# Another order for the dense groups and the expert additions behind the last expert tile

## The reference

```python
xn = layernorm(x)                                     # no weights
h  = layernorm(xn) * g1 + b1
q, k, v = h @ Wq + bq, h @ Wk + bk, h @ Wv + bv       # 16 heads, 4 key/value heads of 8
attn = softmax(rope(q) @ rope(k).T / sqrt(8), window of 32 keys)
x1 = xn + (attn @ v) @ Wo + bo
ff = gelu((layernorm(x1) * g2 + b2) @ Wf1 + bf1) @ Wf2 + bf2     # dense part, 128 -> 512 -> 128
top two of eight experts by xn @ gate.T, weights mult from a jittered softmax
moe = sum over the two of mult * ((silu(xn @ w1[e].T) * (xn @ w3[e].T)) @ w2[e].T)
out = x + (x1 + ff) + moe
```

## Time and profile before

| | |
|---|---|
| median of 3 runs | 522.35 us (519.64 to 522.42) |
| the profiled execution | 519.14 us, span 517.3 us |
| busy, share of the span | TensorE 87%, VectorE 74%, ScalarE 48%, POOL 43% |
| mean granted TensorE clock | 0.927 of 2.4 GHz |
| chain of waits, whole span | TensorE 57%, issue 16%, ScalarE 14%, VectorE 10% |

### The profile page before, as it was taken

The page is one execution under the profiler, slowest core; times in us unless marked ns, Lnnn a source line. Parts: engine busy times, 40 slices in busy tenths (PEclk is TensorE's granted clock), DMA queues, the critical chain, the costliest instruction groups (busy, mean ns, idle before and its releaser), DMA issues.

```text
span 517.3 us, 11263 instructions
## 1 busy us (share of the span) xinstructions
PE 448.0 (87%) x3374; PEld 414.7 (80%) x3375; DVE 382.3 (74%) x1019; ACT 249.6 (48%) x532; POOL 225.0 (43%) x252
## 2 busy tenths in 40 slices
PE   3944976869999999999999999999999999997846
PEld 2834976869989898989898989998989778786533
DVE  6858773776877777777777787867878788577682
ACT  2592004545554555555546464555554564653302
POOL 3630012534555555555555555555544553033110
PEclk9975556998999999999999999999999999999788
DMA  7850022443444544444544343434340500001431
GB/s 221 223 184 0 1 89 80 134 133 103 139 149 123 158 119 151 126 149 120 153 128 154 118 156 116 151 118 155 120 121 2 164 2 0 2 1 61 123 101 41
DMA packets 33667, 56.77 MB, mean 110 GB/s; under 512 B 5967, under 2 KB 21203, under 8 KB 33505
## 3 DMA queue, kind: packets, MB, share of 16 engines
q1 hardware_dynamic: 28160, 47.22, 29.9%
q0 software_dynamic: 4608, 8.93, 5.8%
q10 hardware_dynamic: 864, 0.20, 0.2%
HBM read 47.94 MB, written 8.91 MB: 110 GB/s over the span
## 4 chain that ended last, share of the span: by engine, by line
PE 57%; issue 16%; ACT 14%; DVE 10%; POOL 2%; DVEq 1%; ACTq 0%; POOLq 0%
PE bank L1136 17%; PE bank L1149 11%; PE bank L1100 5%; PE bank L1163 5%; PE bank L1174 4%; PE bank L1099 4%; PE bank L1065 3%; PE bank L1078 3%; ACT qbd L894 3%; ACT act L919 3%; DVE inter L741 2%; ACT gT_sb L871 2%; ACT L918 2%; DVE x_sb L751 1%; ACT act L918 1%
## 5 line engine op out<-in xcount | busy, mean ns | idle before, releaser
L1136 PE MATMUL bank<-xsT,w_sb 128*128 128x128 f32 x1008 | 132.2, 284 | 13.0 <-DVE inter L741 10.2
L1136 PEld LDWEIGHTS bank<-xsT,w_sb 128*128 128x128 f32 x1008 | 120.9, 195 | 18.7 <-issue 17.8
L401 POOL DMA_INDIRECT scratch_ys<-ysb,pair x72 | 77.9, 1082 | 122.5 <-ACT ysb L925 112.1
L394 POOL DMA_INDIRECT xsb<-scratch_xn,token x72 | 73.5, 1021 | 71.2 <-DVE token L572 45.5
L1149 PE MATMUL bank<-w_sb,inter 128*128 x576 | 79.9, 282 | 4.5 <-issue 3.2
L1149 PEld LDWEIGHTS bank<-w_sb,inter 128*128 128x128 f32 x576 | 70.3, 192 | 8.0 <-issue 7.7
L925 ACT ACTIVATE ysb<-bank 128x128 f32<-128x128 f32 x72 | 19.8, 275 | 84.1 <-PE bank L1149 84.1
L1100 PE MATMUL bank<-dv,pO 128*128 128x36 f32 x256 | 49.8, 278 | 1.3 <-ACT h2T_sb L879 1.3
L739 DVE TENSOR_TENSOR inter<-bank,act 64x128 f32<-64x128 f32 x72 | 21.2, 294 | 37.4 <-ACT act L919 32.2
L888 ACT ACTIVATE kT<-bank 32x256 f32<-32x256 f32 x64 | 23.8, 372 | 38.9 <-issue 38.4
L1100 PEld LDWEIGHTS bank<-dv,pO 128*128 128x128 f32 x256 | 39.9, 196 | 2.7 <-issue 2.7
(11 more groups left out here) (147 smaller groups left out, 841.4 us busy)
## 6 DMA issues: line engine op xcount, KB each, us to landing
w_sb<-in_w SPq DMA_DIRECT2D x72, 448.0 KB
w_sb<-scratch_ys SPq DMA_DIRECT2D x8, 512.0 KB, 4.5
scratch_xn<-xn_sb SPq DMA_DIRECT2D x8, 256.0 KB, 3.7
w_sb<-in_w SPq DMA_DIRECT2D x1, 2048.0 KB, 9.2
out_dram<-x_sb SPq DMA_DIRECT2D x8, 256.0 KB, 3.6
xsb<-scratch_xn,token POOLq DMA_INDIRECT x72
scratch_ys<-ysb,pair POOLq DMA_INDIRECT x72
x_sb<-in_x SPq DMA_DIRECT2D x3, 256.0 KB, 4.0
```

Source lines behind the costliest of these rows:

```text
L394: nc.gpsimd.indirect_dma_start(xsb[:, j % 3, :], None, xn, bass.IndirectOffsetOnAxis(ap=token[:, j:j + 1], axis=0)).then_inc(slots_in[j % ...
L401: nc.gpsimd.indirect_dma_start(ys, bass.IndirectOffsetOnAxis(ap=pair[:, j:j + 1], axis=0), ysb[:, j % 3, :], None, bounds_check=2 * NTOK - ...
L1136: last = nc.tensor.matmul(to[:, c % EC * P:(c % EC + 1) * P], w13_sb[:, i % 3, c * P:(c + 1) * P], xsT[:, p, :], start=True, stop=True)
```

## The change

Three of the four tables are written anew with the fourth. Steps 12 to 15 get one dense group each (group 0 to 3; up in places 0 and 1, down in place 4, `finish` in place 5). Groups 4 to 7 come in steps 16 to 18: up(4) at the start of step 16 and down(4) at its end, up(5) at the end of step 17, up(6) at the start of step 18, up(7) in places 4 and 5, and down(5), down(6) and down(7) one after the other in place 6. `add_experts` goes to places of steps 16 to 18. An entry may hold several groups; within a place the expert additions now stand ahead of `finish`; and ScalarE, which had no place 6, gets one.

```diff
-UP_AT = {(MSTEPS, 0): (0, (0, 1)), (MSTEPS, 1): (0, (2, 3)), (MSTEPS, 2): (1, (0, 1)), (MSTEPS, 4): (1, (2, 3)),
-         (MSTEPS + 1, 0): (2, (0, 1)), (MSTEPS + 1, 3): (2, (2, 3)),
-         (MSTEPS + 2, 0): (3, (0, 1)), (MSTEPS + 2, 1): (3, (2, 3)), (MSTEPS + 2, 2): (4, (0, 1)), (MSTEPS + 2, 4): (4, (2, 3)),
-         (MSTEPS + 3, 0): (5, (0, 1)), (MSTEPS + 3, 3): (5, (2, 3)),
-         (MSTEPS + 4, 4): (6, (0, 1)), (MSTEPS + 4, 5): (6, (2, 3)),
-         (MSTEPS + 6, 4): (7, (0, 1)), (MSTEPS + 6, 5): (7, (2, 3))}
-DOWN_AT = {(MSTEPS, 3): 0, (MSTEPS, 5): 1, (MSTEPS + 1, 5): 2, (MSTEPS + 2, 3): 3, (MSTEPS + 2, 5): 4, (MSTEPS + 3, 5): 5,
-           (MSTEPS + 5, 0): 6, (MSTEPS + 6, 6): 7}
-FINISH_AT = {(MSTEPS, 5): 0, (MSTEPS + 1, 2): 1, (MSTEPS + 1, 5): 2, (MSTEPS + 2, 4): 3, (MSTEPS + 3, 1): 4, (MSTEPS + 3, 5): 5,
-             (MSTEPS + 5, 4): 6, (MSTEPS + 6, 6): 7}
-EXPERTS_AT = {(MSTEPS + 3, 4): 0, (MSTEPS + 4, 1): 1, (MSTEPS + 4, 3): 2, (MSTEPS + 4, 5): 3, (MSTEPS + 5, 1): 4, (MSTEPS + 5, 3): 5,
-              (MSTEPS + 6, 4): 6, (MSTEPS + 6, 5): 7}
+UP_AT = {(MSTEPS, 0): (0, (0, 1)), (MSTEPS, 1): (0, (2, 3)), (MSTEPS + 1, 0): (1, (0, 1)), (MSTEPS + 1, 1): (1, (2, 3)),
+         (MSTEPS + 2, 0): (2, (0, 1)), (MSTEPS + 2, 1): (2, (2, 3)), (MSTEPS + 3, 0): (3, (0, 1)), (MSTEPS + 3, 1): (3, (2, 3)),
+         (MSTEPS + 4, 0): (4, (0, 1)), (MSTEPS + 4, 1): (4, (2, 3)), (MSTEPS + 5, 5): (5, (0, 1)), (MSTEPS + 5, 6): (5, (2, 3)),
+         (MSTEPS + 6, 0): (6, (0, 1)), (MSTEPS + 6, 1): (6, (2, 3)), (MSTEPS + 6, 4): (7, (0, 1)), (MSTEPS + 6, 5): (7, (2, 3))}
+DOWN_AT = {(MSTEPS, 4): (0,), (MSTEPS + 1, 4): (1,), (MSTEPS + 2, 4): (2,), (MSTEPS + 3, 4): (3,), (MSTEPS + 4, 5): (4,),
+           (MSTEPS + 6, 6): (5, 6, 7)}
+FINISH_AT = {(MSTEPS, 5): (0,), (MSTEPS + 1, 5): (1,), (MSTEPS + 2, 5): (2,), (MSTEPS + 3, 5): (3,), (MSTEPS + 5, 4): (4,),
+             (MSTEPS + 6, 6): (5, 6, 7)}
+EXPERTS_AT = {(MSTEPS + 4, 2): (0,), (MSTEPS + 4, 4): (1,), (MSTEPS + 5, 2): (2,), (MSTEPS + 6, 3): (3, 4), (MSTEPS + 6, 5): (5, 6, 7)}
@@ def add_experts(i)
-                if i < 6:
+                if i < 4:
                     dve.wait_ge(ff_added, i + 1)
@@ VectorE, def tail(i)
-                    if (k, i) in FINISH_AT:
-                        finish(FINISH_AT[k, i])
-                    if (k, i) in EXPERTS_AT:
-                        add_experts(EXPERTS_AT[k, i])
+                    for group in EXPERTS_AT.get((k, i), ()):
+                        add_experts(group)
+                    for group in FINISH_AT.get((k, i), ()):
+                        finish(group)
@@ ScalarE, def step
                 products(4)
                 tail(5)
+                tail(6)
@@ TensorE, def tail(i)
-                        down(DOWN_AT[k, i])
+                        for group in DOWN_AT[k, i]:
+                            down(group)
```

## The result

The changed kernel takes 529.76 us (median of 4 runs, 526.95 to 530.63), the kernel before 522.34 us beside it: a ratio of 1.0146, 95% interval 1.0111 to 1.0181. It is slower by 7.4 us. The forecast was 518.7 us, that is faster, and its range ended at 524.5: the time went the other way and out of the range.

The account below looks back on a forecast made before the run. TensorE was taken as the bound in steps 12 to 15, with two waits in the drain. Profiled 519.14 - 5.5 (new order) + 3.3 (one clock fall) = 516.9, plus 1.8 for spread: 518.7 us; range 513.5 to 524.5.

Parts of the forecast that it names:

- So I expect one fall there: Step 16, behind the wait before its transposes: one fall of the clock, low for about 6.9 us, 3.3 us lost.
- rival (b): Steps 12 and 14: the clock falls there too, 6.9 us low and 3.4 us lost each, 525.5 us; chance 0.18.
- its sentence on the skill's rule, with 532 us: Steps 13 and 15 would fall too if pauses between short bursts throttle each time: another 6.8 us, 532 us.
- 1.8 had been added: Whole kernel: 1.8 us added for run-to-run spread, as the profiled execution was the fastest of four.
- the stretch at 111.20: Old trace: a pause of 1.20, 1.15 us busy and a pause of 2.30 ended in a clock fall.
- half of the one at 475.10: Steps 12 and 14: argument against clock falls, their waits being half the old kernel's 3.8 us wait in step 16.
- The chain of the steps: Steps 12 to 15: summed links and waits give 17.5, 19.1, 19.1 and 17.8 us.
- The drain: Steps 16 to 18, from 471.0 to the last down product at 508.25 us, against 513.80 before.
- The gain of 5.5 us: Last down product ends at 508.25 us instead of 513.80, before the clock is counted.
- rival (d): End of the kernel: VectorE late with experts(3) to (7), delaying down(7); up to 521 us; chance 0.05.
- pO: Step 16, ahead of `h2(13)`: takes 2.14 us beside a POOL addition, where it takes 1.23 alone.
- The claim that a down product in place 4 leaves the end of the step bare: Steps 13 and 14: down product (3.65 us) ahead of `project` no longer covers VectorE's and ScalarE's turn; 19.1 us a step.

Follow-up runs that it names:

- e6_fill_half: The changed kernel with extra, unread 256-column products filling TensorE's waits in steps 12 to 16: 0.9977 of the kernel before, 509.41 us.
- e5_after: The changed kernel again, unaltered, beside the others of its series: 1.0145 of the kernel before, 518.77 us.
- e10_light: e6_fill_half with its extra products 16 columns wide instead of 256, same counts, places and semaphore waits: 1.0156 of the kernel before.
- e11_before_late_fill: The kernel before with expert additions of groups 4 and 5 moved to step 18 and extra 256-column products in its two long waits: 0.9872 of the kernel before.
- e7_before_fill_half: The kernel before with extra 256-column products in its two long waits, in steps 16 and 18: 0.9891 of the kernel before.
- e3_experts_late: The kernel before with the expert additions of groups 4 and 5 moved from step 17 to step 18, nothing else: 0.9930 of the kernel before.
- e8_down_last_fill: The changed kernel with down products 0 to 3 at step ends, finishes one step later, extra 256-column products in waits and behind project: 0.9826 of the kernel before.
- e9_split: The changed kernel with finishes one step later and down products 0 to 3 halved, between attend's quarters and at step end; no extra products: 0.9842 of kernel before.

## Why the prediction was wrong

**The step that failed is "So I expect one fall there": the number of low stretches.** It booked 3.3 us for one fall, in step 16, of 6.9 us. The profile after has four, of 20.6 us, 10.3 lost. That is 7.0 of the 9.3 us between the sum (-5.5 + 3.3 = -2.2) and the measured +7.1 of the two profiled executions. The case was on the table as rival (b), with a chance of 0.18 and 525.5 us; it was right in kind. Its clock loss was also right in size, 3.3 + 6.8 = 10.1 us for 10.3, but that is luck: the falls in steps 12 and 14 were 3.4 us each for its 6.9, the one in step 16 was 10.3 for 6.9, and it had none in step 15, whose wait was 2.49 us; only its sentence on the skill's rule, with 532 us, asked about steps 13 and 15. That its 525.5 was 4.3 us short of 529.76 comes from the other terms below (2.3), a region that starts 0.7 us later, and a median 2.8 us above the profiled execution where 1.8 had been added. The low stretches are the cause and not only company: filling the waits with dense products takes 9.4 us off (e6_fill_half beside e5_after), and products of 16 columns at the same places take nothing off (e10_light).

What I read wrong was the evidence, not the mechanism. I had the stretch at 111.20, where two pauses with a dense burst between them ended in a fall, and called the steps' waits "half of the one at 475.10". But I weighed each wait alone. Ahead of the falls in steps 12, 14 and 16 stands a stretch of waits, two transposes and the first light products of `attend` (2.89 busy of 4.60 us, 2.70 of 4.40, 0.61 of 3.50), ahead of that in step 15 one wait (0.63 of 3.10). That the light products have a part in it beside the waits is suggested by two falls that had no wait right ahead of them, but 3.07 us (e6_fill_half) and 3.23 us (e11_before_late_fill) of such products; no run changes the light products themselves, so how much is theirs is not shown. Such stretches come in every step of the new order, and which of them falls changes from one execution to the next (four places in one profile, five in another). The Trainium skill, "TensorE: Matmul & The Clock Gate" (section "HAM oscillation"), describes a matmul kernel that is throttled again at every one of its waits, each of them long by itself. e5_after agrees in that every step fell, 30.8 us in five places, and it goes beyond the page: no wait ahead of these falls was over 2.5 us. Had the prediction gone by that rule, it would have said slower.

**The chain of the steps was right, its sizes a little too small.** Less half of the low stretch, the steps took 17.6, 19.3, 19.3 and 18.1 us; forecast 17.5, 19.1, 19.1, 17.8. With the clock held, e6_fill_half has 17.71 for step 12 and 18.19 for step 15. The table load, the key copies and `keep_own` came in the order and at the distances of the old rows.

**The drain was 1.5 us short.** 43.89 less 5.2 is 38.7, forecast 37.3. up(5) and up(6) took 7.62 us (497.93 to 505.55) where I booked 7.0 from a pair of chunks timed alone. Over more chunks in a row a pair takes 1.97 us: the gelus start at 498.99, 500.96 and 502.92 for every second chunk. ScalarE is idle 0.17 or 0.42 us ahead of each, so it is not its 0.69 us alone that sets the pace, but the way there and back, since a chunk waits for the gelu of the chunk before last. The wait ahead of up(7) with its transposes was 1.39 for 1.0, and up(7) 3.79 for 3.5. Together with the steps this is 2.3 us, the other part of the 9.3.

**So the new order doesn't win even at full clock.** The gain of 5.5 us was counted against 116.3 us, in which the old order paid 5.1 us for its own low clock. At full clock the old order takes 111.3 us (measured, e7_before_fill_half), the new one 113.1 (123.4 - 10.3; an estimate from its own rows; e6_fill_half, extra products included, has 117.2 - 3.4 = 113.8). On one chip e6_fill_half takes 509.41 us and e7_before_fill_half 505.16. Of the forecast gain 5.0 us were clock that the old order wastes and the new one was assumed not to; the other 0.5 was less than the 2.3 by which the steps and the drain were short.

**What held.** The last `residual` no longer waits behind expert additions; in the old order that alone is worth 3.8 us (e3_experts_late). down(7) did not wait for `finish(5)`: VectorE had ended the five groups of additions (513.10) before down(5) was finished, so rival (d) did not occur. VectorE's timeline of the changed kernel:

```profile
501.39 11.71 DVE L748 SCALAR_TENSOR_TENSOR x_sb<-w_sb,mult,x_sb 128x128 f32<-128x128 f32 x40
514.56 0.69 DVE L758 TENSOR_TENSOR x_sb<-bank,x_sb 128x512 f32<-128x512 f32 x1 [1.45 <-issue]
```

pO ran beside a POOL addition in each of steps 13 to 16 and took 2.13 to 2.15 us; the forecast had assumed 2.14 for step 16. The claim that a down product in place 4 leaves the end of the step bare is shown by e8_down_last_fill (step 14 in 17.56 us, extra product included, for 19.3) and e9_split (17.12).

**What stays open.** Which of the low stretches falls in which run, and so how the 529.76 us of the median divide over them, can't be told from single profiles. Nor was it tried to shorten ScalarE's part of the chain (the second table load of a step).

## What to carry to other kernels

Before work is moved out of a stretch in which TensorE is full, list what remains there in time order, waits and light products together, and hold it against the rows of your trace ahead of a fall: where such a stretch comes back in every step, a fall may come in each, and half of the low time is to be booked on the path. Compare orders at the same clock: a gain over a kernel that itself loses time to the clock may be nothing but that loss. And a block of dense work cut in two, one half set among the light products and one left as cover (e9_split), took the kernel from 1.0031 to 0.9842 without any extra work, with one fall left in its profile.

## What the runs showed of the hardware that I had not expected

The time lost at the low clock varies from run to run more than the work does: the changed kernel's six runs of one series span 7.4 us (514.68 to 522.05), e7_before_fill_half, with none in the region, 1.4 us (504.14 to 505.56). And an fp32 product of 128x512 is two matmul instructions of 0.43 us, which made two experiments twice as heavy as meant; the count in the timeline (x4 for two chunks of up) had shown it.
